# Edge attention of a graph network: on TensorE the radial products go ahead of the next turn's turned rows

## The reference

```python
def _conv_per_edge(x_src, edge_attr, edge_sh, Wang, Wlin, W1, b1, W2):
    rad = relu(edge_attr @ W1 + b1) @ W2
    g = edge_sh @ Wang.T
    return x_src * g @ Wlin * rad

q = (node_attr @ Wq).reshape(n, H, DQ // H)
x_src = node_attr[src]
k = _conv_per_edge(x_src, edge_attr, edge_sh, Wang_k, Wlin_k, W1k, b1k, W2k)   # 64 columns, 8 heads
v = _conv_per_edge(x_src, edge_attr, edge_sh, Wang_v, Wlin_v, W1v, b1v, W2v)   # 128 columns, 8 heads
alpha = einsum('ehq,qk,ehk->eh', q[dst], Wdot, k)
ealpha = exp(alpha - segment_max(alpha, dst)[dst])
attn = ealpha / segment_sum(ealpha, dst)[dst]
out = segment_sum(attn[..., None] * v, dst).reshape(n, 128) @ Wout
```

## Time and profile before

| | |
|---|---|
| median of 3 runs | 5324.31 us |
| lowest and highest | 5315.24 and 5349.9 us |
| the profiled execution, whole | 5315.98 us |
| its span in the profile | 5314.2 us |
| mean granted PE clock over the span | 0.89 |
| PE, DVE, ACT, POOL busy in the span | 79%, 57%, 36%, 36% |

### The profile page before, as it was taken

One profiled execution on the slowest core, in us unless ns is written; L12 is line 12 of the kernel. 1 busy time (PEld: TensorE's weight loads), 2 busy tenths in 40 slices (PEclk: granted clock), 3 DMA queues, 4 the chain that ended last, 5 costly groups with the idle time before them and its releaser, 6 DMA issues. The chain is left out here.

```text
span 5314.2 us, 73086 instructions
## 1 busy us (share of the span) xinstructions
PE 4215.5 (79%) x26543; PEld 3463.0 (65%) x26543; DVE 3027.4 (57%) x4129; ACT 1934.3 (36%) x2481; POOL 1919.0 (36%) x2002
## 2 busy tenths in 40 slices
PE   4658999999999945777787878788877878777842
PEld 4657999999999843655565656566665656555632
DVE  8985444544443334656666655656655656566634
ACT  5655666666565412222222222222222222222213
POOL 5640000000000055444554554545554554455352
PEclk8879999999999957889989888988888888899965
DMA  7988999999995434444555544555554555455433
GB/s 169 190 186 283 296 294 295 292 299 291 298 295 192 132 88 129 142 144 143 147 152 148 148 142 137 149 148 151 148 145 143 147 149 148 146 148 149 141 115 48
DMA packets 1012831, 944.01 MB, mean 178 GB/s; under 512 B 705677, under 2 KB 811929, under 8 KB 1012339
## 3 DMA queue, kind: packets, MB, share of 16 engines
q1 hardware_dynamic: 952099, 814.71, 52.1%
q0 software_dynamic: 60368, 124.52, 9.8%
HBM read 648.66 MB, written 289.97 MB: 177 GB/s over the span
## 5 line engine op out<-in xcount | busy, mean ns | idle before, releaser
L2313 POOL DMA_INDIRECT feats_hops<-x_table,src_s x1616 | 1547.1, 957 | 1499.7 <-PE e_turn_ps L2421 1046.8
L1286 PE MATMUL acc<-t_wide,scaled 128*128 128x448 f32 x6860 | 1409.2, 367 | 24.3 <-DVE t_wide L1380 24.3
L1286 PEld LDWEIGHTS acc<-t_wide,scaled 128*128 128x128 f32 x6860 | 1284.8, 188 | 129.1 <-DVE scaled L1398 24.7
L1321 ACT CAST t_wide<-t_ring 128x1568 fp32r<-128x1568 uint8 x490 | 737.7, 1506 | 565.0 <-PE acc L1286 542.6
L1380 DVE CAST t_wide<-t_ring 128x1568 fp32r<-128x1568 uint8 x490 | 478.3, 976 | 733.6 <-PE acc L1286 714.0
L2349 PE MATMUL e_turn_ps<-e_weighted,e_spot 128*128 128x128 f32 x3232 | 506.8, 322 | 283.0 <-issue 271.4
L2349 PEld LDWEIGHTS e_turn_ps<-e_weighted,e_spot 128*128 128x128 f32 x3232 | 469.3, 231 | 322.6 <-issue 311.3
L2482 ACT COPY e_out_rows<-e_turn_ps 128x1024 f32<-128x1024 f32 x202 | 204.5, 1012 | 917.6 <-remote 604.9
L1809 POOL MEMSET l_eps<- 128x1 f32 x1 | 0.1, 104 | 1452.6 <-POOLq L1498 1452.6
L2542 DVE TENSOR_TENSOR feats_hops<-e_ring_ps,e_x_t 128x1024 f32<-128x1024 f32 x202 | 247.2, 1224 | 474.2 <-remote 327.7
L2400 PE MATMUL e_ring_ps<-e_wlin_v,e_x_gv 128*128 128x128 f32 x3232 | 457.5, 294 | 48.3 <-issue 43.3
(11 more groups left out here) (272 smaller groups left out, 5080.9 us busy)
## 6 DMA issues: line engine op xcount, KB each, us to landing
t_ring<-adjacency_bytes SPq DMA_DIRECT2D x490, 512.0 KB, 5.7
sums_table<-e_out_rows SPq DMA_DIRECT2D x202, 576.0 KB
q_first<-hop_zeros_q SPq DMA_DIRECT2D x101, 512.0 KB, 5.9
e_sh<-parts_sh SPq DMA_DIRECT2D x404, 128.0 KB
e_ea<-parts_ea SPq DMA_DIRECT2D x404, 128.0 KB
e_q_rows<-q_first SPq DMA_DIRECT2D x404, 128.0 KB
e_same<-same_row SPq DMA_DIRECT2D x404, 128.0 KB
adjacency_bytes<-lists_staged SPq DMA_DIRECT2D x196, 256.0 KB
```

Of the source, the lines that this page charges most:

```text
L1286: mm = nc.tensor.matmul(acc[c][:, 0:n], U[p][:, b, :], wide[m % WIDE_RING][:, lo:lo + n], start=(b == 0 and p == 0), stop=(b == NB - 1 and ...
L1321: nc.scalar.copy(into, of).then_inc(wide_act, 1)
L2313: nc.gpsimd.indirect_dma_start(x_rows[i % XR][:, g * GT + t, :], None, x1_table, bass.IndirectOffsetOnAxis(ap=src_ix[:, at:at + 1], axis=0 ...
```

## The change

PE issues `radial_values` directly behind `values`, and `turn_x` behind it. Nothing else is changed: the same instructions with the same waits, and the other engines' lists are the same.

```diff
                 if on(j):
                     values(i, j)
+                if on(j):
+                    radial_values(i, j)
                 if on(i + 1):
                     turn_x(i + 1, i)
-                if on(j):
-                    radial_values(i, j)
                 if chain_at(i - 2) is not None:
                     turn_weights(chain_at(i - 2), i)
                 if on(i):
```

## The result

The changed kernel took 5133.22 us in the median of 4 runs (5117.48 to 5147.64), the kernel before 5322.7 us in 4 runs beside it: a ratio of 0.964 with an interval of 0.961 to 0.967.

What follows compares the result with a forecast made beforehand. No engine is full in the attention stretch; a loop of waits through the shared `turn_ps` sets the turn. Terms of -118, +53 and zeros sum to -65 us, from 5315.98 to 5251 us; range 5165 to 5370 us.

Steps and rivals of the forecast that it cites:

- term (1): Radial values (L2410) run where PE stands still for L2482 before the turned rows: -118 us, bounds 0 to 177.
- Term (2): Turned rows (L2421) start a set later where PE had no wait; ACT's copy L2505 stays hidden: 0 us.
- Term (3): In 48 turns with weights, nothing covers ACT's copy L2505 before L2367: 1.10 us each, +53 us.
- Term (4): Earlier radial values let DVE's L2574 start earlier, but L2349 waits for ACT's hidden copy: 0 us.
- Rival B: Late completions before L2482 and L2511 grow and take the gain back: 5335 us, chance 0.27.
- Rival C: Turned rows complete late behind fresh radial values, so L2505 is late and hidden waits: 5400 us, chance 0.13.
- Rival D: Less standing still keeps PE's clock higher in the attention stretch, granted clock above 0.88: 5158 us, chance 0.15.
- The prediction's own sign of being wrong: Wrong if the turn is no shorter with the gap filling seen, or a wait in none of its rows appears.

Runs made afterwards that it cites:

- h2: Kernel before with the two value-path weight tables (Wlin_v, W2v) at zero, same instructions, in a quick session: 4339.2 us, ratio 0.999.
- run 16: Not a follow-up run: "run" is a verb here, 16 values' rows and 16 radial rows run beside the wait before L2482.

## Why the prediction was wrong, point by point

- **The step that failed is term (1), "Radial values in the gap".** Its picture is right: L2410 starts right behind L2400, and PE's wait for L2482 fell by 162 us, more than the 100 asked for. But the term counts only the 115 gaps that stood in the trace, 118 us, with the lateness of completions taken as fixed at its places. It is not. The 449.8 us of "remote" wait before L2511, which the prediction names and then lets stand, hung on the radial set's place and went entirely. What of them and of the other rows before L2511 was lateness is 1.73 us a turn, and 0.04 is left. L2482 became later in turn (2.06 to 3.76 us behind L2349's rows), but there values and radial values lie beside it in every turn. So the loop became 0.93 us shorter, 179 us in 192 turns, where the prediction had 65 in all.
- **Term (2), 0: held.** L2505 starts 0.04 us behind L2421's rows, and L2432 has no wait for it.
- **Term (3), +53 us: the price is right and the place is wrong in its net.** The wait before L2367 is 59.9 us in 45 turns where about 60 was foretold, and a quick session shows the bare loss, 60 us. In the session of the result the same turns got 2.32 us shorter, since they had lost the most to a late hidden (3.65 us) and no longer do. A term of +53 us in the sum was a gain of 111 there. The row that says so stands at 3492.80, 7.75 us behind the last one that the prediction used.
- **Term (4), 0: held.** L2349 waited for DVE's L2574 for 7.7 us in all.
- **Rival B** had the better premise, in the mean: the lateness of L2482 and L2511 together is 3.79 us a turn before and 3.80 after, though not within either kind of turn. Its conclusion, that the gain is taken back, is wrong, since the two places are not equal. Beside the wait before L2511 only gates and queries run, and then PE stands still; beside the one before L2482 run 16 values' rows and 16 radial rows that have to run anyway. Its sign didn't come either: the two "remote" waits are 1021.4 us together before and 966.8 after.
- **Rival C** didn't occur: turned rows stayed on time, though radial values stand right in front of them. In 100 of 180 turns they wait for L2482 first; that they are on time in the others too isn't explained here.
- **Rival D** didn't, though its 5158 us are the nearest of the four to what was measured: the granted clock is 0.88 in both. L2349 got back to the full level (2.53 to 2.02 us in the mean), but the turned rows are at the half level more often (1.20 to 1.49 us). PE's standing still just ahead of them wasn't less: 215.7 us of waits before, 249.9 after (183.6 within the radial set, 53.4 and 12.9 before the turned rows).
- **The prediction's own sign of being wrong came**: a wait that stands in none of its rows, the 183.6 us before rows of L2410, which had none.

Had term (1) been a set of 1.43 us out of every turn, with the weights' 53 us (0.28 a turn) kept and lateness only moved, as an estimate it would have read -1.15 us a turn, 221 us in all. Measured are 0.93 us: turned rows to hidden fell by 0.26 instead of 1.15, as PE's rows there run at the half level more often (a row of L2390 takes 835 ns, before 713; of L2421 336, before 301), while L2349's rows give 0.52 and the step from L2482 to the turned rows 0.17 back. The 0.52 hang on modelled row ends, as said above.

**What stays open.** What makes completions late in some sessions and not in others: not the data of the value path, not the kernel, and not the chip number. Also whether it is the radial set itself or the longer run of rows from turned rows to hidden (5.3 us against 4.05) that makes hidden late. Against length alone stands this: in the changed kernel 65 ordinary turns take 5.3 us or more from turned rows to hidden's end, with rows at the half level, and most weights' turns 7.5 to 9.5 us, with the weights' pause in them, and none has a late hidden; of the 90 ordinary turns that take as long before the change, 58 have one by over 1 us. The radial set is also the only one whose products use 64 of the array's 128 rows. Whether that form makes it slow in a late session is untested: no run had other products of the same length in that place, or the radial set in another form.

## What to carry to other kernels

Where waits stand in the trace that no row explains, ask for each which work lies beside it: here a lateness that is paid in every turn was cheapest at the wait that has the most independent work beside it, and an edit that looks as if it filled one gap may decide which wait carries it. Read one turn of each kind to its end, past the rows that the edit touches. And take the kernel's time in more than one session before an order is chosen: here the same edit is worth -3.6% in one and +1.3% in the other.

## What the runs showed of the hardware

- The same program took 4341 us in five sessions and 5323 to 5414 us in the three others, with one core in use. Up to the attention, which starts at 1972 to 1976 us, nothing differs; its rows then last to 4158 us (h2) or 5091 (before), and what follows it takes 186 or 223 us. Within it the granted clock is 1.00 in a quick session and 0.88 in a late one, and the time from the end of PE's rows to their reader differs: 0.04 us for L2482 in a quick session, 3.76 in the mean and over 5.5 us in 15 of its 192 turns in the late session of the changed kernel. The Trainium skill ("Perfetto Trace Analysis", "Tensor Engine Instruction (MATMUL, LD_WEIGHTS)") says that a TensorE row's end is estimated and that other engines see a result only after PSUM's acknowledgement. The late sessions agree as far as other engines start well behind the rows' ends; that the acknowledgement is what takes the time isn't shown, and in the quick ones a reader starts 0.04 us behind them.
- In late sessions PE's small rows are held up one by one. In the earlier trace rows a row of L2410 has a mean of 329 ns with no idle time; in the changed kernel:

```profile
L2410 PE MATMUL e_ring_ps<-e_w2v,e_hid_v 64*128 64x128 f32 x2992 | 344.9, 308 | 185.7 <-issue 183.6
```

  There rows that would start 0.07 us apart start 0.65 to 0.75 us apart in 118 cases (none before, none in a quick session). Before, it is rows of L2400 that do so, in 27 cases, against 5 in the changed kernel. The set takes 2.90 us from its first row to its last, where it took 1.43. That is what PE shows of the lateness: it is stopped in the middle of a set, in the rows above behind 32 rows of L2349 and L2400. What stops it isn't shown.
